# The one-hots of an edge chunk from one two-input comparison of 1024 columns instead of eight one-input comparisons of 128

## What is computed

```python
xn = _layernorm(x)
x = x + gnn(xn, src, dst, ...) + mix(xn)     # two graph attention layers; a linear attention over all nodes
x = x + ffn(_layernorm(x))                   # 16 experts, two per node, then a norm
# each graph attention layer (4 heads of 64 features):
h = (x @ W).reshape(-1, H, C)
e = leaky_relu(alpha_s[src] + alpha_d[dst], 0.2)
ex = exp(e - segment_max(e, dst)[dst])
out = segment_sum(h[src] * (ex / segment_sum(ex, dst)[dst]), dst) + b
```

## Time and profile before

| | |
|---|---|
| median of three executions | 3250.85 us |
| profiled execution, its own time | 3245.28 us |
| span of its instructions | 3243.4 us |
| first edge stage, first to last gather | 189 to 1177 us |
| second edge stage, first to last gather | 1302 to 2290 us |
| granted TensorE clock, mean | 0.817 of full speed |
| busy: TensorE, VectorE, ScalarE, GpSimd | 2010.8, 1836.5, 1005.1, 1859.4 us |

### The profile page before, as it was taken

One profiled execution on the slowest core, in us unless ns is written; L12 is line 12 of the kernel. 1 busy time (PEld: TensorE's weight loads), 2 busy tenths in 40 slices (PEclk: granted clock), 3 DMA queues, 4 the chain that ended last, 5 costly groups with the idle time before them and its releaser, 6 DMA issues. The chain is left out here.

```text
span 3243.4 us, 51573 instructions
## 1 busy us (share of the span) xinstructions
PE 2010.8 (62%) x11139; PEld 1632.5 (50%) x11140; DVE 1836.5 (57%) x5366; ACT 1005.1 (31%) x1903; POOL 1859.4 (57%) x2040
## 2 busy tenths in 40 slices
PE   1837777777777767456666555666670069999600
PEld 0525555555555545345544444545550059999500
DVE  3656666666666653655555555555694024444366
ACT  0524444444444425222222222222130023333222
POOL 0357777777777730777777777777562721111254
PEclk9968888888888888778787888787895579999855
DMA  2734444444444434344444444443466422222265
GB/s 55 223 87 128 127 126 126 126 127 127 126 126 126 126 107 171 91 107 107 107 107 107 107 107 107 107 106 107 144 204 194 155 71 70 70 70 71 70 186 178
DMA packets 266807, 387.84 MB, mean 120 GB/s; under 512 B 85081, under 2 KB 200539, under 8 KB 266609
## 3 DMA queue, kind: packets, MB, share of 16 engines
q0 software_dynamic: 92832, 255.84, 28.5%
q1 hardware_dynamic: 133093, 86.81, 9.5%
q10 hardware_dynamic: 40828, 44.59, 4.0%
HBM read 305.91 MB, written 81.54 MB: 119 GB/s over the span
## 5 line engine op out<-in xcount | busy, mean ns | idle before, releaser
L821 POOL DMA_INDIRECT gathered<-table,idx x1568 | 1499.0, 956 | 625.1 <-issue 497.1
L968 PE MATMUL psA_e<-gathered,hotf 128*128 128x260 f32 x3136 | 962.1, 474 | 11.9 <-DVE gathered L863 11.8
L968 PEld LDWEIGHTS psA_e<-gathered,hotf 128*128 128x128 f32 x3136 | 749.1, 245 | 160.9 <-issue 12.7
L960 PE MATMUL psT<-identb,hot 128*128 128x128 bf16 x1568 | 163.4, 267 | 672.6 <-DVE hot L846 672.6
L863 DVE TENSOR_TENSOR gathered<-gathered,psW_e 128x2048 f32<-128x2048 f32 x196 | 448.2, 2287 | 75.4 <-ACT psW_e L927 75.4
L960 PEld LDWEIGHTS psT<-identb,hot 128*128 128x128 bf16 x1568 | 120.5, 120 | 688.6 <-issue 608.9
L918 ACT ACTIVATE hotf<-hot 128x1024 f32<-128x1024 bf16 x196 | 207.1, 1057 | 765.0 <-DVE hot L846 764.8
L857 DVE TENSOR_TENSOR z_e<-both_e,gathered 128x32 f32<-128x32 f32 x196 | 37.7, 192 | 589.2 <-DMA gathered<-table,idx 589.2
L846 DVE TENSOR_SCALAR hot<-iota,code_r 128x128 bf16<-128x128 bf16 x1568 | 302.4, 287 | 2.2 <-issue 1.2
L1553 POOL DMA_DIRECT2D ys_d<-xo x113 | 61.1, 541 | 381.0 <-DVE xo L1513 381.0
L1493 ACT ACTIVATE w1e<-w 128x1024 f32 x113 | 119.5, 1058 | 409.7 <-PE xpsH L1534 265.0
(11 more groups left out here) (248 smaller groups left out, 2629.9 us busy)
## 6 DMA issues: line engine op xcount, KB each, us to landing
gathered<-table,idx POOLq DMA_INDIRECT x1568
w<-in_L_ffn_w ACTq DMA_DIRECT2D x8, 2048.0 KB, 16.0
xx<-xs_d SPq DMA_DIRECT2D x113, 128.0 KB, 2.0
ys_d<-xo POOLq DMA_DIRECT2D x113, 128.0 KB, 2.0
xs_d<-zero_rows SPq DMA_DIRECT2D x49, 256.0 KB, 2.9
table<-acc POOLq DMA_DIRECT2D x49, 130.0 KB
table<-acc SPq DMA_DIRECT2D x49, 130.0 KB, 1.9
xnT_d<-xnT ACTq DMA_DIRECT2D x49, 128.0 KB, 1.8
```

The lines of the kernel that those rows point to most:

```text
L821: pool.indirect_dma_start(out=G[:, q, k, :], out_offset=None, in_=table, in_offset=bass.IndirectOffsetOnAxis(ap=idx[:, q, k:k + 1], axis=0 ...
L960: ins = pe.transpose(psT[:, k, :], hot[:, q, k, :], identb[:])
L968: ins = pe.matmul(psA[:, par, 0:GW], hotf[:, q, k, :], G[:, q, k, :], start=(k == 0), stop=(k == KT - 1))
```

## The change

The eight comparisons of one input with a scalar per partition become one comparison of two inputs over 8 by 128 columns. Both inputs lie in SBUF: `iota`, read again for each of the eight, and the eight codes of the chunk, each read 128 times. The semaphore `hot` rises by one per chunk, and the two waits count accordingly. Everything else is as it was.

```diff
@@ -842,8 +842,9 @@
             def one_hot(g, c, q, par, use):
-                for k in range(KT):
-                    dve.tensor_scalar(hot[:, q, k, :], iota[:], code_r[:, ds(c * KT + k, 1)], None, ALU.is_equal).then_inc(s["hot"], 1)
+                places = iota[:].rearrange("p (k f) -> p k f", k=1).to_broadcast([P, KT, P])
+                codes = code_r[:, ds(c * KT, KT)].rearrange("p (k f) -> p k f", f=1).to_broadcast([P, KT, P])
+                dve.tensor_tensor(hot[:, q, :, :], places, codes, ALU.is_equal).then_inc(s["hot"], 1)
@@ -913,7 +914,7 @@
             def floats(g, c, q, par, use):
-                act.wait_ge(s["hot"], g * KT + KT)
+                act.wait_ge(s["hot"], g + 1)
@@ -954,7 +955,7 @@
             def turn(g, c, q, par, use):
-                pe.wait_ge(s["hot"], g * KT + KT)
+                pe.wait_ge(s["hot"], g + 1)
```

## The result

The changed kernel takes 3328.7 us, median of 4 runs (3321.8 to 3332.0), against 3252.0 us for the kernel before (4 runs, 3249.6 to 3254.2). The ratio is 1.023, with a 95% interval of 1.021 to 1.025. The medians lie 76.7 us apart. The forecast was 3331 us, 81 more than before, in a range of 3300 to 3360.

What follows compares the result with a forecast made beforehand. GpSimd's unbroken row of gathers was taken to bound the edge stages. Gathers held by the comparison add 83 us and the blend gives back 2: 3250.85 + 81 = 3331 us, range 3300 to 3360.

Steps and rivals of the forecast that it cites:

- The bound: Edge stages: GpSimd issues gathers without pause, 10.0 us a chunk, 1960 of 3243 us; VectorE waits 3.0 us per chunk.
- Part 1, the comparison: VectorE's new 1024-column comparison takes 1.22 us (1.15 to 1.32) instead of 1.54 per chunk; the 62 us saved are worth nothing.
- Part 2, the held gather: Edge stages: a gather wanting its read during the comparison waits for its end; 38 plus 45 us, together +83.
- The two constants read from line 837's neighbours: Start of the edge stages: a gather is held 0.12 us after its start and has 0.82 us left once released.
- Part 3, the give-back: Line 578's blend no longer delays a gather by 0.02 us in over half the chunks: -2 us, at most 4.
- That nothing is held: Rival for the edge stages: the comparison holds no gather and the change is hidden, 3245 to 3251 us; chance 0.10.
- that the eight comparisons hold GpSimd up today: Rival for the kernel before: removing them frees gathers from 0.946 to 0.942 us, 8 us faster, 3243 us; chance 0.03.
- The dearer comparison: Rival for the new VectorE instruction: it runs at half rate, 2.3 us, no chunk escapes, some 3545 us; chance 0.03.
- The signs that the prediction named: Changed profile: one gather in eight at 1.3 to 1.4 us, others 0.946; second-stage chunks 10.4 to 10.5 us; comparison 1.22.
- The row beside line 863: Second stage: a gather beside a 2.29 us weighting with one PSUM input takes 0.94 us, so length alone holds none.
- The pauses of 0.30 us: GpSimd's idle time between gathers, called issue: 497.1 us in 1555 pieces, read as waiting for nothing the profile shows.
- The lower bound of 1.15 us: Comparison time at an ordinary rate, taken from line 837's 3136 columns and 0.08 us overlap; it gives 69 instead of 83.

Runs made afterwards that it cites:

- The copy: The changed kernel with places in PSUM, plus an SBUF-to-SBUF copy of 2000 f32 columns ahead of each comparison: 3381.6 us against 3252.4 for the kernel before.
- the eight comparisons (3250 to 3258 us): Changed kernel with its comparison split into eight of 128 columns, each with two SBUF inputs: 3311.3 us, ratio 1.0171 to the kernel before.

## Why the prediction was right

**The bound.** As argued, GpSimd's row of gathers sets the length of the edge stages. The saving on VectorE (59.6 us less busy over the whole span, 62 forecast) bought nothing in any run. With the places in PSUM the saving is there and the gathers are free, and the ratio is 0.9994. VectorE's wait for gathers grew to 739.9 us, 730 forecast.

**Part 1, the comparison.** 1.215 us against 1.22 taken from line 398. The mix of bf16 and f32, which had opened the bound to 1.32, cost nothing; the bf16 copy of the codes changed nothing either.

**Part 2, the held gather.** The two constants read from line 837's neighbours were 0.12 and 0.82 us; 193 gathers give 0.819 for the second. The sum over the chunks was 38 and 45 us; over their usual 0.946 us the held gathers took 37.6 and 42.5 us more, 80.1 where the forecast had 83. This sum had taken the scatter of VectorE's places against the gathers from the kernel before. In the kernel after 3 chunks pay nothing and 5 over 0.7 us, where the forecast had 11 and 13. The sum came out nearly the same, the distribution did not; that holding a gather itself evens out VectorE's next start would explain it, but no run shows it.

**Part 3, the give-back.** Forecast -2 us. No run isolates it, but the two traces do: the 1560 gathers of the kernel before that don't stand beside line 837 take 1.2 us more than 1560 x 0.946, the 1367 of the kernel after that are neither there nor held 0.7 us less than 1367 x 0.946. That is -1.9 us. Together with the held gathers and 0.2 us of other differences this makes the +78.4 measured, +81 forecast. The remaining 3.5 us lie in the stretches outside the edge stages, where no term of the sum stood.

**What was luck.** The span grew by 81.9 us, where the sum said 81, because 3.5 us that it had no term for stand against 2.6 us too many in the edge stages. Between medians the change is 76.7 us, between profiled executions 81.7, so the 2.3 us between forecast and measured median are less than what single executions differ by. The mechanism is right without this closeness, and doesn't explain it.

**The rivals.** That nothing is held fell with the profile after and with the places in PSUM; that the eight comparisons hold GpSimd up today fell as well, for with them gone and the gathers free the ratio is 0.9994. The dearer comparison fell at 1.215 us. The signs that the prediction named are there: one long gather per chunk, the seven others at 0.946, chunks of 10.49 us.

**Readings that were loose.** The row beside line 863 that was to show that length alone holds no gather is the gather of 1701.91, which began 0.05 us before that instruction and would have been free in any case. The next one shows it, well inside line 863's 2.29 us:

```profile
1703.16 0.94 POOL L821 DMA_INDIRECT gathered<-table,idx  x1 [0.30 <-issue]
```

The pauses of 0.30 us are what 497.1 us in 1555 pieces give once the first, of 23.7 us, is taken out; with it the quotient is 0.32. The lower bound of 1.15 us for the comparison doesn't follow from the rows beside it: 3.34 us for 3136 columns make 1.09 for 1024, 1.17 with the overlap of 0.08. None of this moves the forecast.

**Where the reasons were too narrow.** The law was stated for VectorE instructions with two SBUF inputs. The copy shows that one input is enough when it is read at twice the rate. And "held until the instruction ends" is right for one instruction only: in a row of short ones a waiting gather was passed over 57 times of 98 in the first stage. The forecast did not rest on either, but the expectations of the eight comparisons (3250 to 3258 us) did, and missed by more than 50 us.

## What to carry to other kernels

When GpSimd issues indirect DMAs back to back and sets the length of a stage, look in the trace for the ones that are longer than the median and for the VectorE instruction beside them: a merged, faster VectorE instruction with both operands in SBUF can cost more on GpSimd than it saves. Put one operand of the long ones in PSUM: that removed the 2.3% here, and the same edit to the products of line 837 gave 0.5% in the kernel before, with no instruction made shorter. Splitting the instruction is no safe cure: eight parts still cost 1.7%. And its cost depends on where it falls against the gathers, so anything that shifts VectorE can change it: the same comparison cost nothing in 56 chunks of one run and about 1 us in 5 others.

## What the runs showed of the hardware

- A comparison of 1024 columns with one operand in PSUM and f32 takes 1.215 us, the same as with both in SBUF, one of them bf16.
- A gather of 0.946 us is held at two moments: one 0.12 us after its start (193 gathers ended 0.819 us after the comparison that held them), and one after which 0.12 us are left (66 gathers beside the copy). The first is held by a comparison with two SBUF inputs, both are held by the copy at double rate. That the first is the read of its 128 numbers fits, since it takes a second SBUF input to hold it; what the second is, no run shows.
- The hold begins 0.14 us after the recorded start of the VectorE instruction (the step at 0.617 us in the run with two halves), 0.15 to 0.16 for the single comparison (free when it began 0.03 us before a gather, held at 0.04).
- A waiting gather can be passed over by back-to-back comparisons with two SBUF inputs: 1.79 us in place of 0.95. With two of 512 columns it never was, with eight of 128 in 66 of 196 chunks, and there only when it began at least 0.6 us after the row's start.
- The Trainium skill ("SBUF — State Buffer", section "Who interferes with whom") reports a probe in which two-input instructions did not stall a DMA issued by GpSimd. For the indirect gathers here they do, by 0.4 us per chunk, and the measurement decides.
